# RWKV time mixing and a gated expert layer, on one core: one output projection issued a slot earlier, into a PSUM bank of its own

## What is computed

```python
# attention part, per batch; shifted[t] = x[t-1], shifted[0] = 0
key, value, rec = (x * m + shifted * (1 - m) for m in (mix_key, mix_value, mix_receptance))
k, v, r = key @ Wk, value @ Wv, sigmoid(rec @ Wr)
rwkv = wkv(time_decay, time_first, k, v)      # a running, max-stabilised weighted mean over the tokens
x = layernorm(x + (r * rwkv) @ Wo)
# expert part, per token: 8 experts of 16 hidden units, the 2 best are kept
gate = softmax(x @ router_w.T) * top2_mask
x = layernorm(x + sum_e gate[e] * silu(x @ down_w[e].T) @ up_w[e].T)
```

## Time and profile before

| what | value |
|---|---|
| median of 3 runs | 459.97 us (459.67 to 460.25) |
| the profiled execution's span | 458.2 us, first to last instruction |
| TensorE busy | 444.6 us, 97% |
| VectorE busy | 404.1 us, 88% |
| ScalarE busy | 356.0 us, 78% |
| GpSimd busy | 312.0 us, 68% |
| mean granted TensorE clock | 0.997 |

### The profile page before, as it was taken

One profiled execution on the slowest core, in us unless ns is written; L12 is line 12 of the kernel. 1 busy time (PEld: TensorE's weight loads), 2 busy tenths in 40 slices (PEclk: granted clock), 3 DMA queues, 4 the chain that ended last, 5 costly groups with the idle time before them and its releaser, 6 DMA issues.

```text
span 458.2 us, 6679 instructions
## 1 busy us (share of the span) xinstructions
PE 444.6 (97%) x1984; PEld 340.2 (74%) x1984; DVE 404.1 (88%) x616; ACT 356.0 (78%) x801; POOL 312.0 (68%) x300
## 2 busy tenths in 40 slices
PE   8999999999999999999999999999999999999993
PEld 3444567777888888888888888888888888888761
DVE  5989989899788989999898998989898996876976
ACT  1666757877888779888788888888798887768695
POOL 2355677588658998579858797569966694744334
PEclk9999999999999999999999999999999999999998
DMA  8703230033000042002320042100520022300016
GB/s 239 223 0 117 93 92 1 1 115 93 1 1 0 2 160 92 24 0 74 135 70 0 1 139 93 46 0 24 162 93 1 1 69 94 137 1 0 0 49 229
DMA packets 20244, 30.64 MB, mean 67 GB/s; under 512 B 2032, under 2 KB 7152, under 8 KB 20208
## 3 DMA queue, kind: packets, MB, share of 16 engines
q1 hardware_dynamic: 20208, 30.21, 20.3%
HBM read 21.82 MB, written 8.39 MB: 66 GB/s over the span
## 4 chain that ended last, share of the span: by engine, by line
PE 78%; DVE 5%; ACT 2%; POOL 2%; issue 1%; ACTq 0%; DVEq 0%
PE PH L449 5%; PE PV L330 5%; PE PV L336 5%; PE PV L331 5%; PE PR L336 5%; PE PR L330 5%; PE PK L330 5%; PE PR L331 5%; PE PK L336 5%; PE PK L331 5%; PE PP L359 4%; PE PP L360 4%; PE PP L364 4%; PE PT L431 3%; PE PP L379 2%
## 5 line engine op out<-in xcount | busy, mean ns | idle before, releaser
L592 ACT ACTIVATE PR<-PR 128x512 f32<-128x512 f32 x128 | 74.6, 583 | 29.8 <-PE PR L336 10.6
L1213 POOL TENSOR_TENSOR DQ<-DEN,EX 128x512 f32<-128x512 f32 x32 | 41.3, 1290 | 20.6 <-DVE DEN L871 20.6
L1219 POOL TENSOR_SCALAR NM<-SUM,RS 128x1 f32<-128x1 f32 x30 | 8.0, 267 | 62.1 <-ACT RS L592 62.1
L330 PE MATMUL PK<-KH,WKH 128*128 128x512 f32 x112 | 46.2, 413 | 0.6 <-DVE NUM L888 0.6
L925 DVE SCALAR_TENSOR_TENSOR KT<-D,VEC,XT 128x512 f32<-128x512 f32 x57 | 45.8, 851 | 0.0
L330 PE MATMUL PV<-VH,WVH 128*128 128x512 f32 x112 | 45.6, 407 | 0.0
L336 PE MATMUL PR<-RL,WRH 128*128 128x512 f32 x112 | 44.0, 393 | 0.7 <-POOL RL L1181 0.7
L330 PE MATMUL PR<-RH,WRH 128*128 128x512 f32 x112 | 44.5, 398 | 0.2 <-DVE RW L912 0.2
L336 PE MATMUL PV<-VL,WVH 128*128 128x512 f32 x112 | 43.9, 392 | 0.0
L336 PE MATMUL PK<-KL,WKH 128*128 128x512 f32 x112 | 43.9, 392 | 0.0
L331 PE MATMUL PK<-KH,WKL 128*128 128x512 f32 x112 | 43.8, 391 | 0.0
(11 more groups left out here) (275 smaller groups left out, 1285.7 us busy)
## 6 DMA issues: line engine op xcount, KB each, us to landing
XT<-in_xt SPq DMA_DIRECT2D x32, 256.0 KB, 3.3
XN<-in_x SPq DMA_DIRECT2D x28, 256.0 KB, 2.7
out<-XN SPq DMA_DIRECT2D x28, 256.0 KB, 2.0
X1T<-in_wo SPq DMA_DIRECT2D x1, 1024.0 KB, 5.1
XT<-in_x SPq DMA_DIRECT2D x4, 256.0 KB, 4.2
out<-XT SPq DMA_DIRECT2D x4, 256.0 KB, 2.4
X1T<-in_wk SPq DMA_DIRECT2D x2, 256.0 KB, 4.9
XN<-in_wv SPq DMA_DIRECT2D x2, 256.0 KB, 5.7
```

Source lines behind the costliest of these rows:

```text
L330: eng.matmul(dst[:, :], wh[:, c, o], high[:, c, :], start=(c == 0), stop=False)
L592: eng.activation(*a, **k).then_inc(q[s], 1)
L1213: eng.tensor_tensor(DQ[:, :], DEN[:, 0:T], EX[:, 1, :], ALU.add).then_inc(q["e"], 1)
```

## The change

`project(1)` is issued in slot 4, right behind `project(0)` and ahead of `rec(4)`, and no longer in slot 5. Its result goes to the bank PU, and it no longer waits for `residual(0)`; `residual(1)` reads PU through the same function `projected_at`. `turn(0)` keeps its place in slot 5. No instruction is added or taken away on any engine, and only TensorE's order is changed.

```diff
@@ -141,7 +141,7 @@
         def projected_at(t):
             if t // NT == LAST:
                 return tail_bank(t, PP, PT, PK[0], PH)
-            return (PU if t // NT == LAST - 1 and t % 2 else PP)[:, :]
+            return (PU if t == 1 or t // NT == LAST - 1 and t % 2 else PP)[:, :]
@@ -368,7 +368,7 @@
                 b, n = divmod(t, NT)
                 if t == 0:
                     eng.wait_ge(q["wo"], 16)
-                else:
+                elif t > 1:
                     eng.wait_ge(q["res"], t - (b == LAST - 1 and n > 0))
@@ -516,6 +516,7 @@
                     key(s + 1)
                 if s == C:
                     project(0)
+                    project(1)
                 rec(s)
                 if C - 1 <= s <= C:
                     key(s + 2)
@@ -530,7 +531,7 @@
                     ffn_turn(b - 2)
                 for t in past[:1] if s != C + 1 else []:
                     turn(t)
-                for t in now[:1] if j else []:
+                for t in now[:1] if j and s > C + 1 else []:
                     project(t)
                 for t in past[:1] if s == C + 1 else []:
                     turn(t)
```

## The result

The changed kernel takes 463.69 us (median of 4, 462.70 to 463.84) against 460.11 before (median of 4): the medians are 3.6 us apart. The ratio is 1.0071, with a 95% interval of 1.0059 to 1.0083, which is 3.3 us, as are the means (463.5 against 460.2 us). The forecast was 2.3 us. The direction is as predicted; the time is 0.6 us above the upper end of the range.

A forecast was written before the change was run, and what follows sets the result against it. TensorE, busy 97% of the span, was taken to bound the kernel. Moved work 0, wait removed -1.05, waits added about 3.3: +2.3 us taken, 462.3 us; range 461.4 to 463.1.

The forecast's parts named there:

- The wait taken away, -1.05 us: In rec(4), TensorE's wait for GpSimd's RL disappears: 0.72 us recorded idle plus 0.33 us around it, gaining 1.05 us.
- rec(4) later by 2.38 us, gate(4) with no slack: rec(4) ends 3.43 - 1.05 = 2.38 us later; VectorE's gate(4) and the chain to numerator(5) move by the same.
- The two new waits: TensorE waits about 1.55 us before turn(0) for the normalised tile and 1.7 us before value(6) for numerator(5).
- turn(1), tight by 0.14 us: turn(1) began 0.14 us after normalise(1) ended, so TensorE can't come back below +2.24 us there.
- The clock falls: Rival: TensorE's near-idle 3.7 us halves the clock, value(6) takes up to twice 3.2 us; 465.5 us, chance 0.03.
- the rival in which rec(4) still waits: RL would come later than 67.3 us, so rec(4) keeps its wait: +3.1, 463.1 us, chance 0.02.
- The two rules: Trainium skill's advice: keep the matmul engine busy, and free it where others hold it up; by it, -1.05 us alone.

The follow-up runs named there:

- e2: Kernel before, with one of project(1)'s four matmuls (0.86 us) put ahead of rec(4), the other three left in slot 5: 460.07 us, 1.0000.
- e3: Kernel before, with two of project(1)'s four matmuls (1.72 us) put ahead of rec(4): 460.81 us, 1.0017.
- e5: The changed kernel run again unaltered, for more executions and a profile of a slower one: 463.78 us, 1.0074.
- e4: Changed kernel plus unused idle-time matmuls, six ahead of turn(0) and five ahead of value(6): 462.60 us, 1.0054.
- e9: Changed kernel plus six unused idle-time matmuls ahead of turn(0) only, the wait ahead of value(6) left idle: 462.34 us, 1.0046.
- e8: On e2: scan_max(5) and lead(5) ahead of gate(4), four mixes behind lead(6), VectorE's WOL behind residual(1): 459.51 us, 0.9985.
- e1: Changed kernel with project(1) behind rec(4), ahead of key(6), still in slot 4 and bank PU: 462.40 us, 1.0054.
- e6: On e1, with GpSimd's large subtraction into WOL moved to the end of its slot 5, behind normalise(1): 461.93 us, 1.0039.

## Why the prediction was right in kind and wrong in size

- **The wait taken away, -1.05 us: right.** 3.15 us against 4.21.
- **rec(4) later by 2.38 us, gate(4) with no slack: right.** gate(4) +2.38, VectorE idle 3.61 us (forecast 3.6), ScalarE 6.39 (forecast 6.4). e2 and e3 show the same by dose: 0.0 and +0.7 us for 0.86 and 1.72 us put ahead, where -0.1 and +0.6 to +0.7 follow from the step.
- **The two new waits: right.** 1.53 and 1.35 us recorded, for 1.55 and about 1.7; value(6) +2.26 us, inside 2.21 to 2.38, and turn(1), tight by 0.14 us, takes it to +2.39.
- **"The clock falls", chance 0.03: the step that failed.** The sum of +2.3 us put nothing in for a fall of the clock. The prediction saw the 3.7 us in which TensorE is all but idle, and called the fall unlikely, since at the end of the span the clock stayed at 2.4 GHz for more than 4 us after the last matmul. That row was taken for a rule, though it is one execution. In the changed kernel's own profiled execution the last matmul ended at 452.09 + 1.02 = 453.11 us, and the clock is below full already in the stretch from 455:

```profile
452.09 1.02 PE L501 MATMUL PV<-KT,DQ 128*128 128x512 f32 x2
...
454.00:455.00 1.00, 0.00 (x0) 0.00 (x0) 0.97 (x3) 0.94 (x5) 0.95 (x2) 1.00 0.96 356
455.00:456.00 1.00, 0.00 (x0) 0.00 (x0) 0.93 (x3) 0.62 (x5) 1.00 (x2) 0.72 0.64 242
```

In e5, the same kernel, the last matmul ended at 454.20, and the clock is full up to 457. So the fall comes at different distances in different executions. In the new waits it comes in seven of nine: seen in the profile of e5, and told from the time and the mean clock of the other six. By the runs without a fall (462.6 in e4, 462.3 in e9, 462.7 in two of nine) the mechanism alone lands within 0.4 us of the forecast 462.3.
- **Its price was oversized.** I had +3.2 us for a whole value(6) at half the clock, 465.5 us in all. In e5 seven distances between its matmuls were 0.43 us instead of 0.23 and two a little longer, which is +1.6 us for value(6) and +1.44 us from value(7) on. The two groups of runs of the same kernel are 1.1 us apart, e9 and e5 1.4. With chances the right way round the forecast would have been 462.3 plus 1.1 to 1.6, 463.4 to 463.9 us, and the range should at any rate have reached there.
- **A reading that was wrong without effect.** For the rival in which rec(4) still waits, the third low product was put at 67.3 us. It stands at 68.65, or 68.35 without the 0.30 us of lateness, so that rival was even farther off than it was priced.
- **The two rules.** The Trainium skill, "Perfetto Trace Analysis", section "Optimization Strategies", would have TensorE kept busy, and the engines that hold it up made faster. e2 does only the first, at no gain (0.0 us), so the trace disagrees with it here as long as VectorE's chain is left alone; e8 does the second as well and gains 0.7 us by the medians, which agrees. The Trainium skill, "TensorE: Matmul & The Clock Gate", section "HAM oscillation — how this bites in real kernels", says that a long enough pause between bursts of matmuls sends the clock to half rate; e5 agrees, with 0.50 from 82 to 85 us, and in e4 and e9, with a pause filled, the clock stays full.

That the clock, and not another effect of the filling matmuls, makes the difference is shown for the executions profiled: full clock in e4 and e9, half clock in e5. The others fit by their mean clocks: 0.990 or 0.991 in all seven near 463.7 us, 0.994 to 0.997 in the two near 462.7 and in all of e4 and e9. Why the clock falls in one execution of the changed kernel and not in the next stays open.

## What to carry to other kernels

Work put into a gap of the busiest engine can pay only up to the gap's length, and only if whoever waits for the work behind it has slack. Here the gap was 1.05 us, the work 3.43 us, and VectorE's slack none; even the 0.86 us that fit (e2) gave nothing until VectorE's chain was shortened too (e8). Look for the idle time of the engine that comes next in the chain: 1.21 us of idle time, ended by the product that would be delayed, meant here that every microsecond came through. And where a change leaves TensorE two waits close together, look at the clock in several executions, not in one: six idle-time matmuls in the first wait took about 1.4 us off here (e9 against e5), though an order without the waits is worth more.

## What was not expected of the hardware

- A mix on VectorE, whose two large inputs lie in SBUF, waits for the end of a GpSimd subtraction that runs in SBUF. The waiting is inside its own duration. The mix of slot 5 took 2.84 us beside a subtraction that ended at 82.44 (e1), and 0.75 us in e6, where GpSimd's last had ended at 77.67 + 1.30 = 78.97, just before it began. In the kernel before it took 1.05 us, beside one that ended at 79.16. VectorE's timeline of the kernel before:

```profile
78.66 1.05 DVE L925 SCALAR_TENSOR_TENSOR KT<-D,VEC,XT 128x512 f32<-128x512 f32 x1
79.63 0.68 DVE L900 SCALAR_TENSOR_TENSOR PR<-PR,DQ 128x512 f32<-128x512 f32 x1
```

And GpSimd's:

```profile
77.87 1.29 POOL L1244 TENSOR_TENSOR WRL<-XN,WRH 128x512 fp32r<-128x512 f32 x1
79.12 2.85 POOL L1262 TENSOR_TENSOR WOL<-X1T,WOH 128x1024 fp32r<-128x1024 f32 x1
```

In e1 and in the kernel before the mix ended 0.54 to 0.55 us after the subtraction. gate(5), which reads one input from PSUM, ran beside the next subtraction in its usual 0.68 us. The Trainium skill, "SBUF — State Buffer", section "SBUF: two separate sides", has this as an exclusive lock on a port pair shared by the two engines, held for the whole instruction and not divided; the three durations agree with it. A shift of 0.5 us on VectorE became one of 2.4 us in this way, which no sum over durations of the kernel before gives.
- The clock's fall depends on the execution: of nine executions of the same program seven have its time and mean clock, and the one profiled first was one of the two without.
